# Softmax passes of a graph network: in TensorE's order a step's picks move ahead of the sums of the second group

## The chip, the cores and the metric

The kernel is one program on one core of a Trainium2 chip. The metric is the device time of the whole program in microseconds (us); less is better. A core has TensorE (matrix products; its weight loads are listed apart as PEld), VectorE (DVE), ScalarE (ACT), GpSimd (POOL) and SyncE (SP, which issues transfers). Each engine takes its instructions in the order of its program, and they are tied together by semaphores.

## The reference

Four graph networks run one after the other over the same 3125 nodes and 103,125 edges, which come sorted by destination. Each is followed by a residual sum and a layer norm. The third is the one that matters here. It has three layers, each of them graph attention with 8 heads, a batch norm and a SiLU:

```python
def _gat(x, src, dst, W, a_src, a_dst, bias, n_nodes):
    H, C = a_src.shape
    xw = (x @ W).reshape(n_nodes, H, C)
    al_s = jnp.einsum('nhc,hc->nh', xw, a_src)
    al_d = jnp.einsum('nhc,hc->nh', xw, a_dst)
    logits = jax.nn.leaky_relu(al_s[src] + al_d[dst], LRELU_SLOPE)
    m = jax.lax.stop_gradient(jax.ops.segment_max(logits, dst, num_segments=n_nodes))
    e = jnp.exp(logits - m[dst])
    denom = jax.ops.segment_sum(e, dst, num_segments=n_nodes)
    alpha = e / denom[dst]
    out = jax.ops.segment_sum(alpha[:, :, None] * xw[src], dst, num_segments=n_nodes)
    return out.reshape(n_nodes, H * C) + bias
```

The first two layers have 256 output columns (C = 32), the third 128 (C = 16). All data is fp32.

## The kernel before, in words

The sorted edges are cut into groups of 512 edges that all point into one block of 128 nodes. There are 228 groups; a step takes two of them (1024 edges, 8 tiles of 128), so that a layer's softmax pass (`gat_pass`) has 114 steps, and the three layers have 342. Everything of a step is a chain over four engines:

- POOL (`gather`, L1502) fetches the rows of the source nodes, 8 indirect transfers, two steps ahead of the step whose messages need them.
- ACT (`pack`, L1546) copies the logits' source part out of them. TensorE (`turn`, L1703) transposes it, so that edges lie along the free axis, and DVE (`scan`, L1585) takes a running maximum over each run of edges with one destination. TensorE (`turn_back`, L1709) transposes the maxima back.
- DVE (`run_ends`, L1592) keeps only the value at the end of each run in `ends`. TensorE (`pick`, L1719) multiplies `hot`, the one-hot matrix of the edges' destinations (`edge_hot`, L1577), with `ends`: 8 products of 9 columns, by which each node gets its maximum.
- DVE (`maxima`, L1600 to L1629) raises the running maximum of each node (`top`), works out by how much older sums must fade, and splits al_d and the maximum into three bf16 parts.
- TensorE (`dst_gather`, L1731) brings these parts back to the edges. DVE (`logits`, L1635 to L1644) forms the shifted logits, ACT (`power`, L1558) their exponentials, and DVE (`messages`, L1651) multiplies them into the gathered rows.
- TensorE (`sums(0)` and `sums(1)`, both L1741) sums the messages per node: for each of the two groups of the step 4 products of 264 columns (136 in the third layer) into a PSUM bank of its own. DVE (`add(0)` and `add(1)`) first scales the accumulator of the group's block by the fade (L1673) and then adds the bank (L1677).

The steps overlap. `pipeline` runs one loop on each engine. Its parts carry a lag: in turn t of the loop a part with lag l works on step t - l. The order of the parts in the list is the order of the instructions on that engine, and it is written by hand. In the profile an fp32 product has two records, so that 8 picks are x16 and the 4 products of a group are x8.

DVE's list, and what TensorE has to have finished for its parts:

```python
pipeline(dve, (2, maxima), (1, scan), (2, logits), (1, run_ends), (2, keep_fade), (3, add(0)), (2, messages),
         (3, add(1)), (0, edge_hot), per_turn=RING)
```

`maxima` waits for the picks of its step (made in the turn before), `logits` for `dst_gather` of the same turn, `run_ends` for `turn_back` of the same turn, `add(0)` and `add(1)` for `sums(0)` and `sums(1)` of the same turn. TensorE's parts wait in return: `sums` for the messages of the turn before and for the bank, `dst_gather` for the last instruction of `maxima`, `turn_back` for `scan`, and `pick` for four things:

```python
pe.wait_ge(hot_made, n.total(1, 1))
pe.wait_ge(masked, n.total(1, 2))
pe.wait_ge(flagged, n.total(1, 1))
pe.wait_ge(offered, n.total(1, 1))
```

`masked` is raised by `run_ends` of the same turn. `hot_made`, `flagged` (ACT, L1540) and `offered` (L1603, by which the bank of the picks is free) belong to earlier work.

Of the kernel before, what the change touches and what calls it, by code (L numbers as in the profile page):

```python
# [633 lines left out]
def pipeline(eng, *parts, per_turn=2):  # L634


    last = max(lag for lag, _ in parts)
    head = -(-last // per_turn) * per_turn
    whole = STEPS // per_turn * per_turn

    def at(times):
        for t in times:
            for lag, part in parts:
                if 0 <= t - lag < STEPS:
                    part(Step(None, (t - lag) // per_turn, (t - lag) % per_turn, per_turn))

    at(range(head))
    with eng.Fori(head // per_turn, whole // per_turn) as turn:
        for r in range(per_turn):
            for lag, part in parts:  # L650
                part(Step(turn, (r - lag) // per_turn, (r - lag) % per_turn, per_turn))
    at(range(whole, STEPS + last))
# [794 lines left out]
def gat_pass(nc, m, layer):  # L1447


    _, c, wide, full, both = gat_columns(layer)  # L1450
    RING, TWO = 4, 2
    ROWS = BATCH * HEADS
    with Stage(nc, f"gat{layer}") as st:
# [35 lines left out]
        def blocks_of(eng, n):  # L1489
            _, ids = nc.values_load_multi_w_load_instructions(m.block_tab[0:1, n.group(size=PAIR)], engines=[eng.engine],  # L1490
                                                              min_val=0, max_val=NB - 1)
            return ids

        with nc.Block() as block:
            @block.gpsimd
            def _(pool):
                def gather(n):
                    pool.wait_ge(index_in[n.q], n.count(16, 16))
                    pool.wait_ge(msg_made, n.total(1, 1))
                    pool.sem_inc(passed, 1)  # L1500
                    for j in range(BATCH):
                        pool.indirect_dma_start(rows[n.q][:, j, :], None, table,  # L1502
                                                bass.IndirectOffsetOnAxis(ap=index[n.q][:, j:j + 1], axis=0))\
                            .then_inc(gathered[n.q], 16)

                pipeline(pool, (0, gather), per_turn=RING)
# [189 lines left out]
            @block.tensor  # L1696
            def _(pe):
                def turn(n):
                    q = n.of(TWO)
                    pe.wait_ge(packed, n.total(1, 1))  # L1700
                    pe.wait_ge(scanned, n.total(1, TWO))
                    pe.sem_inc(turn_passed, 1)
                    pe.transpose(turn_ps[0:ROWS, 0:P], al_s[q][:, :, :].rearrange("p b h -> p (b h)"), m.ident[:, :]).then_inc(turned, 1)  # L1703

                def turn_back(n):
                    q = n.of(TWO)
                    pe.wait_ge(scanned, n.total(1, TWO + 1))
                    pe.wait_ge(masked, n.total(1, 1))
                    pe.matmul(back_ps[:, 0:ROWS], run_max[q][:, :], m.ident[0:ROWS, 0:ROWS], start=True, stop=True)\  # L1709
                        .then_inc(backed, 1)  # L1710

                def pick(n):
                    q = n.of(TWO)
# [4 lines that stand above are left out]
                    for j in range(BATCH):  # L1718
                        ins = pe.matmul(pick_ps[:, j * (HEADS + 1):(j + 1) * (HEADS + 1)], hot[n.q][:, j, :], ends[q][:, j, :],  # L1719
                                        start=True, stop=True)  # L1720
                    ins.then_inc(picked, 1)

                def dst_gather(n):
                    q = n.of(TWO)
                    size = PARTS * 2 * HEADS
                    pe.wait_ge(dst_hot[q], n.seen(TWO, 1, 1))
                    pe.wait_ge(shown, n.total(1, 1))
                    pe.wait_ge(parted, n.total(1, 1))
                    pe.wait_ge(joined, n.total(1, 1))
                    for j in range(BATCH):  # L1730
                        ins = pe.matmul(row_ps[:, j * size:(j + 1) * size], dhot[q][:, j * P:(j + 1) * P],  # L1731
                                        parts[q][:, j // GROUP, :, :].rearrange("p k h -> p (k h)"), start=True, stop=True)
                    ins.then_inc(dst_rows, 1)

                def sums(g):
                    def part(n):
                        q = n.of(TWO)
                        pe.wait_ge(msg_made, n.total(1, RING + 1))
                        pe.wait_ge(added, n.total(PAIR, g + 1))
                        for j in range(GROUP):  # L1740
                            ins = pe.matmul(sum_ps[g][:, 0:wide], hot[n.q][:, g * GROUP + j, :], msg[q][:, g * GROUP + j, :],  # L1741
                                            start=j == 0, stop=j == GROUP - 1)
                        ins.then_inc(summed, 1)
                    return part

                pe.sem_inc(turned, RING)
                pe.sem_inc(backed, TWO)
                pe.sem_inc(picked, TWO)
                pe.sem_inc(dst_rows, TWO)
                pe.sem_inc(summed, PAIR * RING)  # L1750
                pipeline(pe, (1, turn), (3, sums(0)), (2, dst_gather), (1, turn_back), (3, sums(1)), (1, pick), per_turn=RING)


def destination_gather(pe, m, n, dhot, table, width, bank, done):
# [326 lines left out]
```

## Time and profile before

| what | value |
|---|---|
| median of 3 runs | 10514.31 us (10507.37 to 10517.66) |
| the profiled execution | 10513.72 us, of which the span is 10511.4 us |
| TensorE, matrix products busy | 7135.4 us (68%) |
| VectorE busy | 5278.9 us (50%) |
| GpSimd busy | 6605.8 us (63%) |
| ScalarE busy | 1896.1 us (18%) |
| softmax passes, first to last `turn_back` | 4868.8 to 9071.8 us, the layers' node work between them |
| mean granted clock of TensorE over the span | 0.626 of full speed |

The span runs from the first to the last instruction; 2.3 us lie around it. The shares are means over stages that have different limits, so the softmax passes have to be read by themselves. The three passes fill some 40% of the span. A granted clock of 1.0 is 2.4 GHz, one of 0.5 is 1.2 GHz.

### The profile page before, as it was taken

The page shows a single profiled execution, that of the slowest core. Times are in us where ns is not written, and L with a number is a line of the kernel's source. Part 1 is how long each engine was busy: PE and PEld are TensorE (multiplying, and loading weights), DVE is VectorE, ACT ScalarE, POOL GpSimd, SP SyncE. Part 2 cuts the span into 40 slices and gives each one's busy share as a digit, 9 for nine tenths or more (in the row PEclk, how much of TensorE's full clock was granted, in tenths as well). Part 3 has the DMA queues.
Part 4 walks back from the last instruction along what each step waited for, and adds up shares of the span by engine and source line. Part 5 has one row for each costly group of instructions (what it writes and reads, how often), then busy time and mean ns, then how long its engine had stood idle before and what let it go on. Part 6 is the DMA issues. An engine that isn't in the chain of part 4 may idle for free. (4 is left out here: it accounts for less than half of the span.)

```text
span 10511.4 us, 139346 instructions
## 1 busy us (share of the span) xinstructions
PE 7135.4 (68%) x31465; PEld 6194.0 (59%) x31466; DVE 5278.9 (50%) x13681; ACT 1896.1 (18%) x4610; POOL 6605.8 (63%) x6850
## 2 busy tenths in 40 slices
PE   0266666666665555547888877888877888688887
PEld 0256565555553444434666655666666777678887
DVE  1233332333332222234777765777756777544444
ACT  0000000000001111112222222222223333222222
POOL 0277775777773777713666634666627777367776
PEclk9855655555556777755666676666665555555555
DMA  0122221222221222203444423444424444244443
GB/s 9 43 58 59 57 59 40 62 59 57 58 54 38 60 60 60 60 21 97 142 141 141 141 85 119 141 141 141 141 64 111 113 111 113 56 116 120 120 120 102
DMA packets 685282, 917.39 MB, mean 87 GB/s; under 512 B 429785, under 2 KB 469403, under 8 KB 685094
## 3 DMA queue, kind: packets, MB, share of 16 engines
q0 software_dynamic: 233472, 500.97, 18.5%
q1 hardware_dynamic: 450726, 414.73, 13.2%
q10 hardware_dynamic: 1024, 1.05, 0.0%
q8 instruction: 18, 0.29, 0.0%
q14 instruction: 42, 0.34, 0.0%
HBM read 899.55 MB, written 17.37 MB: 87 GB/s over the span
## 5 line engine op out<-in xcount | busy, mean ns | idle before, releaser
L1502 POOL DMA_INDIRECT gat_rows<-xw_table,gat_index x2736 | 2590.4, 947 | 1933.8 <-issue 824.6
L1741 PE MATMUL bank<-gat_msg_s,gat_hot 128*128 128x264 f32 (+1 forms) x5472 | 1918.2, 522 | 106.7 <-DVE gat_msg_s L1651 106.6
L1741 PEld LDWEIGHTS bank<-gat_msg_s,gat_hot 128*128 128x128 f32 x5472 | 1394.9, 296 | 377.7 <-issue 110.7
L828 PE MATMUL bank<-gcn_rel,gcn_rhot 100*128 100x64 f32 x3648 | 836.3, 424 | 1019.7 <-DVE gcn_rhot L794 1019.7
L828 PEld LDWEIGHTS bank<-gcn_rel,gcn_rhot 100*128 100x128 f32 x3648 | 794.5, 330 | 1077.2 <-issue 588.3
L683 POOL DMA_INDIRECT gcn_rows<-x_table,gcn_index x912 | 1017.0, 1115 | 276.5 <-issue 257.0
L683 POOL DMA_INDIRECT gcn_rows<-in_x,gcn_index x912 | 1007.7, 1105 | 276.7 <-issue 257.4
L683 POOL DMA_INDIRECT msg_rows<-pre_table,msg_index x912 | 945.9, 1037 | 277.4 <-issue 258.2
L683 POOL DMA_INDIRECT att_rows<-pre_table,att_index x912 | 943.1, 1034 | 276.8 <-issue 254.2
L1719 PEld LDWEIGHTS bank<-gat_ends_s,gat_hot 128*128 128x128 f32 x5472 | 1004.3, 276 | 37.4 <-issue 4.2
L1719 PE MATMUL bank<-gat_ends_s,gat_hot 128*128 128x9 f32 x5472 | 950.1, 312 | 3.3 <-DVE gat_ends_s L1592 3.3
L802 DVE TENSOR_TENSOR gcn_comp_s<-gcn_rows,bank 128x512 f32<-128x512 f32 x228 | 156.7, 687 | 1453.6 <-DMA gcn_rows<-in_x,gcn_index 728.5
L730 PE MATMUL bank<-gcn_msg_s,gcn_hot 128*128 128x128 f32 x3648 | 821.9, 417 | 23.8 <-DVE acc L742 23.8
L730 PEld LDWEIGHTS bank<-gcn_msg_s,gcn_hot 128*128 128x128 f32 x3648 | 785.6, 326 | 24.8 <-issue 24.8
L730 PE MATMUL bank<-msg_msg_s,msg_hot 128*128 128x129 f32 x1824 | 411.8, 416 | 547.2 <-ACT msg_msg_s L1082 547.2
L730 PEld LDWEIGHTS bank<-msg_msg_s,msg_hot 128*128 128x128 f32 x1824 | 381.3, 318 | 574.0 <-DVE acc L742 553.8
L1651 DVE TENSOR_TENSOR gat_msg_s<-gat_rows,bank 128x2112 f32<-128x2112 f32 (+1 forms) x342 | 680.8, 1991 | 0.4 <-issue 0.4
L1098 DVE TENSOR_TENSOR msg_pre_s<-msg_rows,bank 128x512 f32<-128x512 f32 x228 | 146.4, 683 | 856.5 <-DMA msg_rows<-pre_table,msg_index 850.9
L1731 PEld LDWEIGHTS bank<-gat_parts,gat_dhot 128*128 128x128 bf16 x2736 | 128.3, 113 | 740.0 <-issue 738.8
L1731 PE MATMUL bank<-gat_parts,gat_dhot 128*128 128x48 bf16 x2736 | 160.7, 210 | 581.9 <-DVE gat_parts L1629 415.2
L1759 PE MATMUL bank<-kvq,att_dhot 128*128 x1824 | 418.4, 424 | 148.6 <-ACT att_dhot L716 115.1
L1759 PEld LDWEIGHTS bank<-kvq,att_dhot 128*128 128x128 f32 x1824 | 397.6, 330 | 181.6 <-issue 181.6
(293 smaller groups left out, 10442.0 us busy)
## 6 DMA issues: line engine op xcount, KB each, us to landing
gat_dst<-dst_rows SPq DMA_DIRECT2D x342, 512.0 KB
gcn_ids<-rel_rows SPq DMA_DIRECT2D x228, 400.0 KB
att_dst<-dst_rows SPq DMA_DIRECT2D x114, 512.0 KB, 4.0
gat_rows<-xw_table,gat_index POOLq DMA_INDIRECT x2736
att_attr<-in_edge_attr SPq DMA_DIRECT2D x228, 128.0 KB
gcn_rows<-in_x,gcn_index POOLq DMA_INDIRECT x912
gcn_rows<-x_table,gcn_index POOLq DMA_INDIRECT x912
msg_rows<-pre_table,msg_index POOLq DMA_INDIRECT x912
```

Of the source, the lines that this page charges most:

```text
L683: pool.indirect_dma_start(self.rows[n.q][:, j, :], None, self.table, bass.IndirectOffsetOnAxis(ap=self.index[n.q][:, j:j + 1], axis=0))\
L730: ins = pe.matmul(place(banks, g, width), hot[:, g * GROUP + j, :], msg[:, g * GROUP + j, 0:width], start=j == 0, stop=j == GROUP - 1)
L802: dve.tensor_tensor(comp[q][:, :, :], g.rows[q][:, :, :], rel_ps[q][:, :].rearrange("p (b d) -> p b d", b=BATCH), ALU.mult)\
L828: ins = pe.matmul(rel_ps[q][:, j * DIM:(j + 1) * DIM], rhot[q][:, j * P:(j + 1) * P], rel[:, :], start=True, stop=True)
L1098: dve.tensor_tensor(pre[q][:, part, :], g.rows[q][:, part, :], edge_ps[q][i][:, :].rearrange("p (j d) -> p j d", j=GROUP), ALU.add)\
L1502: pool.indirect_dma_start(rows[n.q][:, j, :], None, table, bass.IndirectOffsetOnAxis(ap=index[n.q][:, j:j + 1], axis=0))\
L1651: dve.tensor_tensor(msg[q][:, :, :].rearrange("p b (h e) -> p b h e", h=HEADS), rows[n.q][:, :, 0:wide].rearrange("p b (h e) -> p b h e", ...
L1719: ins = pe.matmul(pick_ps[:, j * (HEADS + 1):(j + 1) * (HEADS + 1)], hot[n.q][:, j, :], ends[q][:, j, :], start=True, stop=True)
L1731: ins = pe.matmul(row_ps[:, j * size:(j + 1) * size], dhot[q][:, j * P:(j + 1) * P], parts[q][:, j // GROUP, :, :].rearrange("p k h -> p ( ...
L1741: ins = pe.matmul(sum_ps[g][:, 0:wide], hot[n.q][:, g * GROUP + j, :], msg[q][:, g * GROUP + j, :], start=j == 0, stop=j == GROUP - 1)
L1759: ins = pe.matmul(bank[:, j * width:(j + 1) * width], dhot[:, j * P:(j + 1) * P], table[:, ds(b, 1), :].rearrange("p o w -> p (o w)"), sta ...
```

## The change

Only the order of TensorE's parts in `gat_pass` changes. `pick` (lag 1) and `sums(1)` (lag 3) trade places, so that a turn runs turn, sums(0), dst_gather, turn_back, pick, sums(1). No instruction is added or taken away, and no wait is changed.

```diff
@@ -1748,7 +1748,7 @@
                 pe.sem_inc(picked, TWO)
                 pe.sem_inc(dst_rows, TWO)
                 pe.sem_inc(summed, PAIR * RING)
-                pipeline(pe, (1, turn), (3, sums(0)), (2, dst_gather), (1, turn_back), (3, sums(1)), (1, pick), per_turn=RING)
+                pipeline(pe, (1, turn), (3, sums(0)), (2, dst_gather), (1, turn_back), (1, pick), (3, sums(1)), per_turn=RING)
```

## Rows read from the trace of the kernel before

**Rows 1.** Busy time by stretch in the first and third softmax pass, and granted clock.
```profile
core 0: us, PE busy (x) PEld busy (x) DVE busy (x) ACT busy (x) POOL busy (x), PEclk, DMA share, GB/s
5000.00:6200.00 1200.00, 976.20 (x4358) 784.09 (x4357) 944.00 (x2837) 353.40 (x1016) 761.51 (x804) 0.69 0.48 141
...
8000.00:9000.00 1000.00, 823.19 (x4176) 777.41 (x4177) 752.91 (x2719) 337.14 (x970) 738.11 (x783) 0.50 0.41 112
```

**Rows 2.** The same view for the messages (L1651) alone: DVE busy, times.
```profile
5000.00:6200.00 1200.00, 237.29 (x102) 0.69 0.48 141
...
8000.00:9000.00 1000.00, 124.09 (x97) 0.50 0.41 112
```

**Rows 3.** DVE's waits from 4850 to 9100 us: total us, times, longest.
```profile
DVE acc L1673 <- issue: 376.3, 340, 1.4
DVE gat_drow L1635 <- PE bank L1731: 119.0, 316, 3.3
...
DVE gat_pen L1600 <- PE bank L1719: 9.0, 5, 2.6
...
DVE acc L1677 <- PE bank L1741: 7.2, 6, 1.9
```

**Rows 4.** Timeline, first layer, DVE: start, us, instruction, xcount, idle before.
```profile
5224.76 0.56 DVE L1635 TENSOR_REDUCE gat_drow<-bank 128x128 f32<-128x384 f32 x1 [0.23 <-PE bank L1731]
...
5226.04 0.22 DVE L1592 TENSOR_TENSOR gat_ends_s<-bank,run_end 128x64 f32<-128x64 f32 x1
...
5228.32 2.35 DVE L1651 TENSOR_TENSOR gat_msg_s<-gat_rows,bank 128x2112 f32<-128x2112 f32 x1
...
5231.11 0.43 DVE L1677 TENSOR_TENSOR acc<-acc,bank 128x264 f32 x1
5231.45 1.22 DVE L1577 TENSOR_TENSOR gat_hot<-bank,dst_l 128x1024 f32<-128x1024 f32 x1
```

**Rows 5.** Timeline, first layer, TensorE, parts of several turns.
```profile
5224.37 0.36 PE L1731 MATMUL bank<-gat_parts,gat_dhot 128*128 128x48 bf16 x8 [1.46 <-DVE gat_parts L1629]
...
5225.02 2.05 PE L1741 MATMUL bank<-gat_msg_s,gat_hot 128*128 128x264 f32 x8
...
5230.80 3.88 PE L1741 MATMUL bank<-gat_msg_s,gat_hot 128*128 128x264 f32 x8 [1.45 <-DVE gat_msg_s L1651]
...
5237.30 3.41 PE L1741 MATMUL bank<-gat_msg_s,gat_hot 128*128 128x264 f32 x8
5240.55 1.85 PE L1719 MATMUL bank<-gat_ends_s,gat_hot 128*128 128x9 f32 x16
5242.25 0.28 PE L1703 MATMUL bank<-ident,gat_al_s 128*64 128x128 f32 x1
...
5272.58 3.89 PE L1741 MATMUL bank<-gat_msg_s,gat_hot 128*128 128x264 f32 x8
5276.26 3.42 PE L1719 MATMUL bank<-gat_ends_s,gat_hot 128*128 128x9 f32 x16
```

**Rows 6.** Timeline, third layer, TensorE and DVE, one turn.
```profile
8309.65 0.47 PE L1731 MATMUL bank<-gat_parts,gat_dhot 128*128 128x48 bf16 x8 [2.01 <-issue]
...
8310.16 0.56 DVE L1635 TENSOR_REDUCE gat_drow<-bank 128x128 f32<-128x384 f32 x1 [0.18 <-PE bank L1731]
...
8310.67 2.18 PE L1741 MATMUL bank<-gat_msg_s,gat_hot 128*128 128x136 f32 x8
...
8311.57 0.23 DVE L1592 TENSOR_TENSOR gat_ends_s<-bank,run_end 128x64 f32<-128x64 f32 x1
...
8312.64 3.42 PE L1719 MATMUL bank<-gat_ends_s,gat_hot 128*128 128x9 f32 x16
...
8315.17 0.30 DVE L1677 TENSOR_TENSOR acc<-acc,bank 128x136 f32 x1
...
8315.91 0.40 PE L1703 MATMUL bank<-ident,gat_al_s 128*64 128x128 f32 x1
...
8316.11 2.02 PE L1741 MATMUL bank<-gat_msg_s,gat_hot 128*128 128x136 f32 x8
```

## The prediction

> **What bounds the kernel now.** I first read busy time by stretch inside the three softmax passes [rows 1], since the means over the whole span mix stages. In the first pass TensorE is busy 976 of 1200 us and DVE 944; in the third 823 and 753 of 1000. None is full, so the view doesn't yet name a bound. The same view for the messages alone gives the number of turns [rows 2]: 102 in 1200 us is 11.8 us a turn, 97 in 1000 us is 10.3 us.
>
> Next I read DVE's waits over all three passes [rows 3]. The largest is "issue" before L1673, 376.3 us in 340 turns, 1.1 us each: DVE waits there for no other engine. The only steady wait for TensorE is that of the logits for `dst_gather`, 119.0 us over some 340 turns, 0.35 us each. For picks DVE waited 5 times (9.0 us), for sums 6 times (7.2 us). So DVE, in its written order, sets the length of a turn, and TensorE delivers both picks and sums before DVE comes to them. TensorE is the one that waits: 1.46 us before `dst_gather` and 1.45 us before `sums(0)` [rows 5]. The question is therefore not what TensorE gains in free time, but whether each of its results is still there when DVE wants it.
>
> Last I read the timeline around the two parts that trade places [rows 4 to 6]. In the first layer `sums(1)` runs right behind `turn_back`, from 5225.02 for 2.05 us, so it ends at 5227.07; `add(1)` takes it at 5231.11, 4.0 us later. In the third layer it ends at 8310.67 + 2.18 = 8312.85 and is taken at 8315.17, 2.3 us later. The picks end last on TensorE in a turn, and nothing waits for them until `maxima` of the next turn.
>
> **The change part by part.** It adds and removes no instruction and no transfer, and alters no wait; the two parts keep their durations at a given clock. What moves is where waits stand in TensorE's queue.
>
> 1. *The picks have to wait where they stood free.* `pick` needs `masked`, which `run_ends` (L1592) raises in the same turn. DVE does `run_ends` behind the logits; it ends at 5226.04 + 0.22 = 5226.26 in the first layer and at 8311.80 in the third [rows 4, 6]. TensorE is through with `turn_back` when `sums(1)` starts now, at 5225.02 and 8310.67. So TensorE stands still for some 1.2 us a turn where it works on sums today. The other three waits of `pick` (the one-hot matrix, ACT's flags, the free bank) are for work of the turn before or of the head of this one, and cost nothing. ACT, POOL and SP don't come into it: no queue of theirs is reordered.
>
> 2. *`sums(1)` comes behind that wait and behind the picks.* I count from the end of `run_ends`. To `add(1)` it is 5231.11 - 5226.26 = 4.85 us in the first two layers, and 8315.17 - 8311.80 = 3.37 us in the third. That much time TensorE has for both parts. It needs:
>  - the handover from DVE to TensorE, 0.13 us (messages end at 5230.67, the sums that wait for them start at 5230.80 [rows 4, 5]); I take 0.1;
>  - the picks, start to the next part's start: 8315.91 - 8312.64 = 3.27 us at 1.2 GHz [rows 6], 5242.25 - 5240.55 = 1.70 us at 2.4 GHz [rows 5];
>  - `sums(1)` to its end: 3.89 us at the low clock and 2.05 us at the high one in the first two layers [rows 5], 2.18 us at the low clock in the third [rows 6].
>
> 3. *Third layer.* The granted clock is 0.50 throughout [rows 1]. 0.1 + 3.27 + 2.18 = 5.55 us against 3.37: `add(1)` starts 2.2 us later each turn. Behind it on DVE stand `edge_hot` and all of `maxima` of the next turn, hence `dst_gather`, the logits and `run_ends`: the whole loop moves by that much. Both parts run together in 112 of the 114 turns (picks have lag 1, sums lag 3), so 112 x 2.18 = 244 us.
>
> 4. *First and second layer.* Here the granted clock is 0.69 on average, and it depends on it. Both parts slow: 0.1 + 3.27 + 3.89 = 7.26, which is 2.4 us late. Fast picks, slow sums: 5.69, 0.84 late. Slow picks, fast sums: 5.42, 0.57 late. Both fast: 3.85, in time. Which is it? Today the clock goes up behind a long block of sums: slow sums of 3.41 us at 5237.30, then fast picks of 1.85 us at 5240.55 [rows 5]. The picks profit from the sums ahead of them. In the new order they have ahead of them a wait for `maxima`, the short `dst_gather` and `turn_back`, and the wait for `run_ends`. And picks don't raise the clock by themselves, as the third layer shows: there TensorE works almost without a gap from 8309.65 to 8318.13, 8.5 us, and stays at 1.2 GHz [rows 1, 6]. The block that raises it will be `sums(1)`, turn, `sums(0)`, which then stand together; the rise comes in time for `sums(0)`, which nobody is in a hurry for, and will mostly be lost in the two idle stretches that follow. I weigh both slow with 8 in 10 and the two mixed cases with 1 in 10 each: 0.8 x 2.4 + 0.1 x 0.84 + 0.1 x 0.57 = 2.06 us. 2 x 112 turns make 461 us. The ends are 0 (both fast, always) and 2.4 x 224 = 540 us.
>
> The Trainium skill (TensorE: Matmul & The Clock Gate, "Why this matters for your kernels") advises keeping TensorE continuously busy to get the high clock. By it the new block of picks, sums, turn and sums would be fast, and the first two layers would lose nothing, 244 us in all in place of 705. The third layer of this trace speaks against it: 8.5 us of such work stayed slow. I go by the trace and keep the page's outcome as part of a rival.
>
> 5. *Given back.* TensorE must still end `sums(0)` before the next `dst_gather`. At the low clock a turn of it is 1.02 + 1.2 + 0.1 + 3.27 + 3.7 + 0.5 + 3.9 = 13.7 us (`dst_gather` and `turn_back` from 8309.65 to 8310.67, the wait, the handover, the picks, 3.7 for `sums(1)` to the start of the next part by 5272.58 to 5276.26, some 0.5 for turn and its handover, `sums(0)`; [rows 5, 6]), against 11.8 + 2.4 = 14.2 on DVE's side, so DVE keeps the bound, just. The picks are ready earlier, but DVE waited for them 9.0 us in all [rows 3]: no gain. POOL, busy 738 of 1000 us with its gaps of issue beside [rows 1], gets more room in a longer turn.
>
> **Sum.** The profiled execution took 10513.7 us (span 10511.4 and 2.3 around it), 0.6 us under the median of 10514.3. 10513.7 + 244 + 461 = 11,219; I say 11,220 us, 6.7% slower.
>
> **The rivals.**
>
> *The clock mix of today survives* (0.19). The page's rule works in part: the long block keeps the clock up often enough that either the picks or the sums are fast in the first two layers. For it: fast and slow picks both occur today with idle stretches around them [rows 5]. Against it: step 4. With 0.57 to 1.5 us a turn late, 128 to 336 us, and 244 for the third layer, the time is 10,886 to 11,094; about 10,990.
>
> *TensorE becomes a second bound* (0.04). If `dst_gather` has to wait for `sums(0)`, a turn in the first two layers gets still longer than 14.2 us. 0.5 us more is 112 us: 11,330. Against it: the 0.5 us of room in step 5.
>
> *The order doesn't matter* (0.02). `sums(1)` would have to end before DVE wants it in every layer: within 4.85 us, and within 3.37 us in the third. There the slow picks alone with the handover take 3.37, so the clock would have to rise there too. Time 10,514.
>
> *Faster* (0.02). The full clock holds through the whole turn in all three layers. Then picks and sums need 3.85 us in the first two, and in the third about half of 5.55, 2.9, both in time, and the logits no longer wait for a slow `dst_gather`: from its start to L1635 it is 0.39 us when fast [rows 4, 5] and 0.51 us when slow [rows 6]. 0.12 x 336 turns = 40 us: 10,474. It decides only from the point where the third layer leaves 1.2 GHz, which it never does today [rows 1].
>
> **How the numbers follow.** My forecast, both slow in most turns, holds 0.73: with 1.6 to 2.45 us a turn in the first two layers and 2.0 to 2.3 in the third, 10513.7 + 358 + 224 = 11,096 to 10513.7 + 549 + 258 = 11,320. The range for 8 in 10 takes in half of the first rival: 10,960 to 11,330. A difference under 0.2%, some 21 us, can't be told from none in this kernel. All cases but the last two are slower: faster 0.02, same 0.02, slower 0.96.
>
> **What would show it.** In the waits of DVE a new large one stands before L1677, released by TensorE's L1741: some 2.2 us x 112 turns in the third layer and some 2 us x 224 in the others, against 7.2 us now. TensorE waits some 1.2 us before L1719, put down to L1592. In the timeline the order is L1709, gap, L1719, L1741, L1703, L1741. Turns last 12.5 us in the third layer and 13.9 in the first two. The slow picks (3.42 us) are the rule in the first two layers too; if they last 1.85 us mostly, step 4 is wrong and the time is nearer 10,990. If L1677 doesn't wait, step 2 is wrong, and with it the sign.

## The result, and the profile after

The changed kernel takes 11262.08 us in the median (4 runs, 11256.08 to 11264.59) beside 10515.99 us for the kernel before: the ratio is 1.071, 95% interval 1.0692 to 1.0729. The forecast was 11,220 us, range 10,960 to 11,330. One thing has to be known to read what follows: on the chips that ran the experiments e1 to e7, e11 and e12 the kernel before itself took 12,700 to 13,080 us, so each of those runs is compared with before on its own chip, and otherwise by stretches of its trace.

The profiled execution of the changed kernel has a span of 11261.6 us. DVE's waits over the three passes, which answer to [rows 3]:

```profile
DVE acc L1677 <- PE bank L1741: 821.5, 342, 2.7
DVE acc L1673 <- issue: 376.3, 340, 1.4
...
DVE gat_drow L1635 <- PE bank L1731: 85.1, 265, 3.4
...
DVE gat_pen L1600 <- PE bank L1719: 8.1, 4, 2.6
```

The wait of `add(1)` for `sums(1)` has grown from 7.2 us to 821.5 us, 2.4 us in each of 342 turns. What else DVE waits for inside the passes is as before or a little less: the 1.1 us of issue before L1673 are the same 376.3 us, and the logits wait 34 us less for `dst_gather`.

The timeline of TensorE in the first layer (answers to [rows 5]; columns as there):

```profile
5209.93 0.36 PE L1731 MATMUL bank<-gat_parts,gat_dhot 128*128 128x48 bf16 x8 [2.73 <-DVE gat_parts L1629]
5210.22 0.43 PE L1709 MATMUL bank<-ident,gat_run_max 64*128 64x64 f32 x2
5212.02 3.32 PE L1719 MATMUL bank<-gat_ends_s,gat_hot 128*128 128x9 f32 x16 [1.37 <-issue]
5215.19 3.87 PE L1741 MATMUL bank<-gat_msg_s,gat_hot 128*128 128x264 f32 x8
5218.85 0.41 PE L1703 MATMUL bank<-ident,gat_al_s 128*64 128x128 f32 x1
5219.06 1.98 PE L1741 MATMUL bank<-gat_msg_s,gat_hot 128*128 128x264 f32 x8
5223.96 0.36 PE L1731 MATMUL bank<-gat_parts,gat_dhot 128*128 128x48 bf16 x8 [2.92 <-DVE gat_parts L1629]
```

And DVE in the same turn (answers to [rows 4]):

```profile
5211.69 0.23 DVE L1592 TENSOR_TENSOR gat_ends_s<-bank,run_end 128x64 f32<-128x64 f32 x1
...
5219.10 0.43 DVE L1677 TENSOR_TENSOR acc<-acc,bank 128x264 f32 x1 [2.44 <-PE bank L1741]
5219.44 1.22 DVE L1577 TENSOR_TENSOR gat_hot<-bank,dst_l 128x1024 f32<-128x1024 f32 x1
```

`run_ends` is over at 5211.92, the picks start at 5212.02, `sums(1)` at 5215.19 and ends at 5219.06, and DVE takes it at 5219.10: 7.18 us behind `run_ends`, where before it was 4.85. The picks and the first sums run at 1.2 GHz or nearly so (3.32 and 3.87 us, where at 1.2 GHz throughout they take 3.4 to 3.6 and 3.87 to 3.89 in both kernels); only the sums behind them, which are `sums(0)` and for which nobody waits, run at 2.4 GHz (1.98 us). TensorE then stands for 2.9 us, until DVE's `maxima` is through.

This turn is not an exception. In the 85 turns of 5000 to 6200 us the picks take 2.77 to 3.56 us, `sums(1)` 3.40 to 3.87, and the wait of L1677 is 1.88 to 2.68 us long, 2.44 in the mean. In each of them DVE starts L1677 0.03 or 0.04 us behind the end of `sums(1)`. The trace also has a turn in the second layer in which the picks were fast:

```profile
6691.60 1.92 PE L1719 MATMUL bank<-gat_ends_s,gat_hot 128*128 128x9 f32 x16 [1.33 <-issue]
6693.38 3.60 PE L1741 MATMUL bank<-gat_msg_s,gat_hot 128*128 128x264 f32 x8
6697.01 0.43 DVE L1677 TENSOR_TENSOR acc<-acc,bank 128x264 f32 x1 [0.76 <-PE bank L1741]
```

Picks and sums take 1.92 and 3.60 us here, 1.91 less together than the 3.56 and 3.87 of a turn at 1.2 GHz, and the wait is 0.76 us in place of 2.67: 1.91 less. So their length goes over into the wait one for one. By this row some 1.6 us of a turn's loss in the first two layers are the picks' low clock (an estimate: 3.56 - 1.92). Of the 214 turns of these two layers that I could read, 2 have picks under 2.5 us, both in the second layer.

A turn of the third layer (answers to [rows 6]), TensorE:

```profile
8702.86 3.56 PE L1719 MATMUL bank<-gat_ends_s,gat_hot 128*128 128x9 f32 x16 [1.12 <-issue]
8706.27 2.16 PE L1741 MATMUL bank<-gat_msg_s,gat_hot 128*128 128x136 f32 x8
8708.22 0.42 PE L1703 MATMUL bank<-ident,gat_al_s 128*64 128x128 f32 x1
```

and DVE:

```profile
8708.47 0.30 DVE L1677 TENSOR_TENSOR acc<-acc,bank 128x136 f32 x1 [2.43 <-PE bank L1741]
```

The turns' lengths follow from one line per stretch, the messages alone (us of the stretch, DVE busy, times; answers to [rows 2]):

```profile
5000.00:6200.00 1200.00, 201.60 (x86) 0.71 0.41 119
8500.00:9500.00 1000.00, 102.37 (x80) 0.58 0.34 92
```

From the first to the last start of these messages it is 5002.2 to 6197.9 us over 85 turns and 8503.3 to 9497.0 over 79: 14.07 and 12.58 us a turn. Before it was 5003.3 to 6199.7 over 101 and 8004.1 to 8993.5 over 96: 11.85 and 10.31. In the second layer the same reading gives 14.03 us (6666.5 to 7844.7 over 84) against 11.86 (6567.7 to 7599.6 over 87). The differences, (2.22 + 2.17 + 2.27) x 112 = 746 us, are the whole loss (746 us).

### The profile page after: what moved, and what is told of

It is laid out like the page before. It is cut to its first block and busy times, and to the rows that moved or that the text cites. A ratio compares the mean times of both kernels' runs of the same rounds, so it can differ in the third digit from the quotient of the medians.

```text
span 11261.6 us, 139346 instructions
## 1 busy us (share of the span) xinstructions
PE 7226.2 (64%) x31465; PEld 6312.9 (56%) x31466; DVE 5275.9 (47%) x13681; ACT 1895.6 (17%) x4610; POOL 6617.5 (59%) x6850
## 5 line engine op out<-in xcount | busy, mean ns | idle before, releaser
L1741 PE MATMUL bank<-gat_msg_s,gat_hot 128*128 128x264 f32 (+1 forms) x5472 | 1829.0, 504 | 10.3 <-DVE gat_msg_s L1651 10.3
L1719 PE MATMUL bank<-gat_ends_s,gat_hot 128*128 128x9 f32 x5472 | 1183.0, 355 | 412.9 <-issue 409.6
L1719 PEld LDWEIGHTS bank<-gat_ends_s,gat_hot 128*128 128x128 f32 x5472 | 1160.3, 322 | 457.2 <-issue 457.2
L1731 PE MATMUL bank<-gat_parts,gat_dhot 128*128 128x48 bf16 x2736 | 135.8, 192 | 937.7 <-DVE gat_parts L1629 692.0
L1651 DVE TENSOR_TENSOR gat_msg_s<-gat_rows,bank 128x2112 f32<-128x2112 f32 (+1 forms) x342 | 680.9, 1991 | 0.4 <-issue 0.4
L1677 DVE TENSOR_TENSOR acc<-acc,bank 128x264 f32 (+1 forms) x684 | 263.2, 385 | 851.6 <-PE bank L1741 821.5
```

The costliest lines, as they stand in the source:

```text
L1651: dve.tensor_tensor(msg[q][:, :, :].rearrange("p b (h e) -> p b h e", h=HEADS), rows[n.q][:, :, 0:wide].rearrange("p b (h e) -> p b h e", ...
L1677: dve.tensor_tensor(dst_acc, dst_acc, sum_ps[g][:, 0:wide].unsqueeze(1), ALU.add).then_inc(added, 1)
```

## The experiments

**The changed kernel and the kernel before, again (e8, e9).** No edit; they give a second chip for the main result, and the measure for e10.

> The changed kernel itself, unaltered, beside the kernel before on a chip where before takes some 12,700 to 13,100 us. The undisturbed turns should be those of the first comparison: 13.9 us in the first two layers, 12.4 in the third. In turns that are stretched by late instructions of TensorE, part of the 2.2 us is covered. Theory: the ratio is 1.03 to 1.057 (400 to 746 us). If the ratio is under 1.01, the loss belongs to the first chip's timing and not to the order.

> The kernel before, unaltered, for its trace on this chip: the measure for the turns of the other experiments. The shortest quarter of its turns should lie at 11.7 us and 10.2 us, as in the trace shown first; what stretches the others should be gaps of TensorE put down to issue, and results of TensorE that reach DVE late.

On this chip before takes 10490.37 us and nothing is stretched. The changed kernel takes 11230.99 us, ratio 1.0704 (1.0686 to 1.0722). The expectation of 1.03 to 1.057 had reckoned with a stretched chip and doesn't meet this case; the loss is the full one, so it isn't the first chip's alone. The changed kernel by itself was never timed on a chip where before takes 12,700 us or more. The kernel before gave 10490.4 us in its profiled execution; its turns are 11.85 and 10.31 us in the mean, as in the trace shown first, and none of the stretching that e9 was to explain is there.

**Work that needs no sums put into the wait (e10).** The changed kernel, and in DVE's list:

```diff
 ...
-(3, add(0)), (2, messages), (3, add(1)), (0, edge_hot)
+(3, add(0)), (2, messages), (0, edge_hot), (3, add(1))
```

> The changed kernel with DVE's edge_hot ahead of add(1), so that 1.2 us of work that needs no sums lie in the wait. Theory (DVE stands before add(1), in its own order): the wait of L1677 falls from 2.4 to some 1.3 us a turn in undisturbed turns. The loads of the block numbers for maxima then stand behind a short instruction and show some 0.8 us of issue before L1600, so that the turn shrinks by 0.2 to 1.0 us: 13.0 to 13.8 us in the first two layers. Rival (TensorE's own row of work sets the turn): the wait of L1677 stays at 2.4 us less nothing, and the turn gets no shorter, or 0.7 us longer.

It takes 11187.87 us, ratio 1.0663 (1.0646 to 1.0681), 43 us less than the changed kernel on the same chip. DVE's waits in the first layer, 5000 to 6200 us, first of e10:

```profile
DVE acc L1677 <- PE bank L1741: 116.3, 87, 1.5
...
DVE gat_pen L1600 <- issue: 82.5, 87, 1.3
```

then of e8, the changed kernel:

```profile
DVE acc L1677 <- PE bank L1741: 210.1, 86, 2.7
...
DVE gat_pen L1600 <- issue: 6.7, 22, 0.3
```

The wait falls from 2.44 to 1.34 us a turn, by 1.1 us, as `edge_hot` is 1.2 us long. Of that some 0.9 us come back as issue before L1600 (82.5 us in 87 turns, where e8 has 6.7 us): `maxima` loads its block numbers there, and `edge_hot` no longer stands just ahead of it. Net 43 / 336 = 0.13 us a turn, less than the 0.2 to 1.0 expected. TensorE's program is the same in both, and `sums(1)` is taken at the same distance behind `run_ends` (7.20 us in the mean, 7.18 in the changed kernel of the result); what DVE does before it asks for the bank shortens the wait. The fall of the wait alone doesn't rule out that TensorE's own row of work sets the turn, since a gain of 0.13 us is near to none. TensorE's waits rule it out: in the changed kernel it stands for 1.3 us before the picks and for 2.7 us before `dst_gather`, in every turn, and both times for DVE.

**The wait without the picks (e1, e5).** The kernel before, with a part `await_ends` that only waits:

```diff
 ...
-(1, turn_back), (3, sums(1)), (1, pick)
+(1, turn_back), (1, await_ends), (3, sums(1)), (1, pick)
 ...
+def await_ends(n):
+    pe.wait_ge(masked, n.total(1, 2))
```

> The order of before, but TensorE waits for run_ends (masked) ahead of sums(1); the picks stay behind the sums. The wait of the change without its swap. Theory (DVE's add(1) has to wait for sums(1) only because the slow picks stand ahead of it): sums(1) now ends 0.1 + 3.89 = 4.0 us behind run_ends, inside the 4.85 us that DVE leaves (third layer 2.3 of 3.37), so L1677 doesn't wait. The picks end later instead, at 7.2 us at the low clock, where maxima wants them at 6.7 (third layer 5.5 against 4.9): some 0.5 us a turn in perhaps half of the 336 turns. 10,600 us, 10,520 to 10,700, far under 11,262. Rival (it is TensorE standing still for 1.2 us a turn that costs, whatever comes behind it): the same 2.2 us a turn as in the changed kernel, about 11,250.

> The same kernel as e1, since on the chip of that call the kernel before itself took 13,080 us and its turns were stretched by waits that the runs shown first don't have. Where the kernel before takes 10,515 us the theory gives, as for e1, 10,600 us (10,520 to 10,700) and no wait of L1677 for sums; the rival, by which TensorE's standing still costs by itself, about 11,250.

Beside before on the same chips it is no slower: 12914.16 us, ratio 0.9885 (0.983 to 0.9939), and 12721.17 us, ratio 0.9998 (0.9969 to 1.0026). As ratios the theory had said 1.01 and the rival 1.07; both lie above the intervals, the rival far above. The changed kernel by itself has no time on these chips; the nearest is e3 below, the changed order with filling, with 1.0267 on the chip of e1. DVE in a turn of e5 without long gaps:

```profile
6907.12 0.22 DVE L1592 TENSOR_TENSOR gat_ends_s<-bank,run_end 128x64 f32<-128x64 f32 x1
...
6912.51 0.43 DVE L1677 TENSOR_TENSOR acc<-acc,bank 128x264 f32 x1
6914.53 0.17 DVE L1600 TENSOR_SCALAR gat_pen<-bank 128x8 f32<-128x8 f32 x1 [0.46 <-PE bank L1722]
```

and TensorE, where the sums of `sums(1)` stand on L1744 and the picks on L1722:

```profile
6907.39 3.89 PE L1744 MATMUL bank<-gat_msg_s,gat_hot 128*128 128x264 f32 x8 [1.20 <-DVE gat_ends_s L1592]
6911.07 3.42 PE L1722 MATMUL bank<-gat_ends_s,gat_hot 128*128 128x9 f32 x16
```

TensorE stands for 1.20 us, about as long as in the changed kernel, and runs at the low clock too. `sums(1)` ends at 6911.28, and L1677 starts at 6912.51 without waiting. What is late now are the picks, by 0.46 us. Between 5800 and 7000 us of e5, L1677 waits in 25 of 73 turns (60.9 us), and in the others not at all; long waits in some of the turns are there in e4 too, which has TensorE's order of before. In e3 and e11, which have the changed order, it waits in all 66 turns of the same stretch (174.0 and 172.2 us). So the wait for `run_ends` by itself costs next to nothing here; it is the wait with the picks behind it.

**Half of the picks ahead (e2, e6).** `pick` cut in two, 4 of the 8 products in each part:

```diff
 ...
-(1, turn_back), (3, sums(1)), (1, pick)
+(1, turn_back), (1, pick_first), (3, sums(1)), (1, pick_rest)
```

> Turn_back, the waits of pick, 4 of the 8 picks, sums(1), the other 4 picks. Theory: what stands ahead of sums(1) counts by its length. sums(1) ends at 0.1 + 1.64 + 3.8 = 5.5 us against 4.85, 0.7 late; third layer 0.1 + 1.64 + 2.18 = 3.9 against 3.37, 0.55 late: 224 x 0.7 + 112 x 0.6 = 224 us, so 10,740 us (10,650 to 10,850), less than a third of the change's loss. Rival (TensorE's idle time itself): all of it, about 11,250. Rival (a loss in proportion to the picks moved): half, 10,890.

> The same kernel as e2, for the same reason. Theory (what stands ahead of sums(1) counts by its length against the room that DVE leaves): 10,740 us (10,650 to 10,850), with L1677 waiting some 0.6 us a turn. Rival by idle time: about 11,250. Rival in proportion to the picks moved: 10,890.

12664.63 us, ratio 0.9691 (0.9637 to 0.9745), and 12491.42 us, ratio 0.9824 (0.9775 to 0.9873): on these chips faster than before, where the theory had said a ratio of 1.02 and both rivals more. As forecasts of the time all three failed, and why it gains isn't settled. What the trace does show is the wait. A turn of e6 in the first layer, TensorE (L1715 the picks, L1747 the sums):

```profile
6799.45 1.85 PE L1715 MATMUL bank<-gat_ends_s,gat_hot 128*128 128x9 f32 x8 [1.34 <-issue]
6801.15 3.87 PE L1747 MATMUL bank<-gat_msg_s,gat_hot 128*128 128x264 f32 x8
```

and DVE:

```profile
6805.05 0.43 DVE L1677 TENSOR_TENSOR acc<-acc,bank 128x264 f32 x1 [1.01 <-PE bank L1747]
```

With half the picks ahead, 1.85 us, L1677 waits 1.01 us, where all of them, 3.3 us, make it 2.4 us, and none of them none. In the turns around it the wait is 0.53, 0 and 1.02 us, which is the some 0.6 us expected; in the turn without a wait the half took 1.29 us and the sums 3.44. The picks' length goes over into the wait as soon as the room is used up, as the theory has it.

**The clock (e3, e11).** The changed kernel with products that nobody reads in TensorE's gaps: 5 and 2 in e3, 7 and 3 in e11.

```diff
 def pick(n):
 ...
+    pe.wait_ge(offered, n.total(1, 1))
+    fill(pick_ps, 3)
 ...
     pe.wait_ge(masked, n.total(1, 2))
 ...
 def dst_gather(n):
 ...
+    pe.wait_ge(joined, n.total(1, 1))
+    fill(row_ps, 7)
     pe.wait_ge(dst_hot[q], n.seen(TWO, 1, 1))
```

The waits for `offered` and `joined`, by which the two banks are free, move ahead of the filling.

> The changed kernel, with products into unused columns of TensorE's own banks that nobody reads: 5 of 128 columns ahead of dst_gather's wait for maxima, 2 ahead of pick's wait for run_ends. No work of the chain is changed. Theory: of the 2.2 us a turn the greater part is the low clock at which the picks and sums(1) run behind two idle stretches. With the stretches filled the clock should stay at 1.0 in the first two layers: 0.1 + 1.70 + 2.05 = 3.85 against 4.85, no wait at L1677, and at full clock in the third about 2.9 against 3.37. About 10,520 us; if the clock rises in part only, up to 10,900. Rival (the order costs by the positions of the waits, whatever the clock): 11,260 or more, since TensorE has more to do.

> As e3, with more filling: in the changed kernel, 7 products of 128 columns that nobody reads ahead of dst_gather's wait and 3 ahead of the wait of the picks, which is some 1.8 and 0.8 us at the high clock, in gaps of 2.9 and 1.3 us. Theory (without the low clock the picks and sums(1) fit in the room that DVE leaves): the clock stays near 1.0, L1677 waits for next to nothing, 10,500 to 10,600 us where before takes 10,500. If the clock rises in part, 10,600 to 10,950. Rival (positions alone, whatever the clock): as the changed kernel, 11,230 us, or more by the filling.

13428.79 us, ratio 1.0267 (1.0205 to 1.0329), and 13463.95 us, ratio 1.0334 (1.0281 to 1.0387). This is neither the theory's time nor an answer for it. TensorE in e11 (L1714 the filling, L1724 the picks):

```profile
6519.54 0.36 PE L1737 MATMUL bank<-gat_parts,gat_dhot 128*128 128x48 bf16 x8 [0.20 <-issue]
...
6520.19 0.94 PE L1714 MATMUL bank<-ones,ident 128*128 128x128 f32 x6
6525.65 3.55 PE L1724 MATMUL bank<-gat_ends_s,gat_hot 128*128 128x9 f32 x16 [4.53 <-issue]
```

and DVE:

```profile
6524.04 0.56 DVE L1635 TENSOR_REDUCE gat_drow<-bank 128x128 f32<-128x384 f32 x1 [4.33 <-remote]
```

The filling ran at the high clock (6 records in 0.94 us), but DVE saw the result of `dst_gather` 4.3 us late, and in that gap the clock fell again: the picks took 3.55 us as ever. The chip alone doesn't explain this lateness. DVE's waits from 5800 to 7000 us, first in e3, then in e1 on the same chip, without filling:

```profile
DVE gat_drow L1635 <- remote: 272.0, 65, 4.9
```

```profile
DVE gat_drow L1635 <- PE bank L1734: 19.0, 67, 0.4
```

It stands in all but one turn of e3 and likewise in e11 (277.1 us in 65), while e1 has it in 3 turns (8.7 us). So it came with the filling, or with the filling on such a chip. Why is open. What the filling was to test, fast picks in every turn, was therefore not measured; the only evidence is the turns of the changed kernel in which the picks happened to be faster, shown under the result.

**Block numbers of `add` loaded early (e4, e7, e12).** The order of before; on DVE a part `add_ids` with the load ahead of `maxima`:

```diff
-pipeline(dve, (2, maxima), (1, scan),
+pipeline(dve, (3, add_ids), (2, maxima), (1, scan),
 ...
```

> The order of before. DVE loads the two block numbers of add at the head of the turn, ahead of maxima, behind edge_hot's 1.2 us, in place of right ahead of add(0), where 1.1 us a turn stand as issue. Theory (DVE's own list sets the turn): up to 1 us a turn less in the first two layers, until TensorE, which waits for DVE some 2 us of 11.8, or GpSimd sets it; in the third GpSimd has 8 x 1.25 = 10.0 of 10.3 us, so little: 10,514 - 0.8 x 224 - 0.2 x 112 = 10,310 us (10,270 to 10,500). Rival (TensorE bounds the turn already): no change.

> The same kernel as e4 (the order of before; DVE loads add's two block numbers at the head of the turn), again because the kernel before took 13,080 us beside e4. Theory (DVE's own list sets the turn): where before takes 10,515 us, 10,310 us (10,270 to 10,500); turns of the first two layers 10.9 to 11.5 us against 11.8. Rival (TensorE bounds the turn already): no change.

> As e4 and e7, which gave ratios of 0.981 and 0.980 on chips where before took some 13,070 us: the order of before, with add's block numbers loaded at the head of the turn. Where before takes 10,500 us: turns of 11.4 to 11.7 us in the first two layers (what the shortest quarter showed in e4 and e7, against 11.5 to 11.75 of before), so the gain is 0.1 to 0.4 us a turn: 10,400 to 10,480 us. If DVE alone set the turn it would be 1 us a turn and 10,230.

12801.05, 12785.54 and 12793.28 us, with ratios of 0.9806 (0.9751 to 0.9861), 0.9798 (0.9758 to 0.9837) and 0.9814 (0.9764 to 0.9864). It beat the kernel before three times, by 2%, the ratio that e4's theory had for it, but only on chips where before takes some 13,000 us; where before takes 10,500 us it wasn't measured. The 1.1 us of issue before L1673 went, and 0.76 us of it came back before `maxima`. Two turns of e12, the picks and L1600 in each:

```profile
6961.18 1.85 PE L1720 MATMUL bank<-gat_ends_s,gat_hot 128*128 128x9 f32 x16
6965.03 0.17 DVE L1600 TENSOR_SCALAR gat_pen<-bank 128x8 f32<-128x8 f32 x1 [0.76 <-issue]
...
6973.00 3.42 PE L1720 MATMUL bank<-gat_ends_s,gat_hot 128*128 128x9 f32 x16
6976.64 0.17 DVE L1600 TENSOR_SCALAR gat_pen<-bank 128x8 f32<-128x8 f32 x1 [0.76 <-PE bank L1720]
```

The second wait is put down to the picks, which end at 6976.42. But in the turn before they were over at 6963.03, 2.0 us early, and the same 0.76 us stand there as issue. So it is the loads, now twice as many behind `edge_hot`, that take this time; that TensorE would be the next bound close behind is not shown.

## Why the prediction was right

*Step 1, the picks have to wait.* Right: 1.37 us before L1719 in the turn shown of the first layer and 1.26 in the mean, 1.12 in the third, against 1.2 forecast. I had said that the profile would put it down to L1592; it puts it down to issue. That the picks start 0.1 us behind `run_ends` in every turn shows the releaser.

*Step 2, the count from `run_ends`.* The mechanism is right, one term was too small. Where both parts run at 1.2 GHz the count is 7.41 us, not 7.26, and in the third layer 5.70, not 5.55. The picks take 3.41 us to the next part's start (8702.86 to 8706.27), where I had 3.27 from the kernel before. That the turn shown comes to 7.18 is because its picks are a little faster. e5 and e6 agree that neither the wait alone nor the number of products decides, but the length ahead of `sums(1)` against the room that DVE leaves.

*Step 3, third layer.* 2.18 us forecast, 2.27 measured: 254 us for 244. `add(1)` is 5.70 - 3.37 = 2.33 us later, and the logits wait 0.05 us less.

*Step 4, first two layers.* The mechanism is right, the weights were too mild: 2.06 us forecast, 2.22 and 2.17 measured, 492 us for 461. I had given the mixed cases 2 turns in 10; of the 85 turns of 5000 to 6200 us none has fast picks or a fast `sums(1)`. So `add(1)` is 7.18 - 4.85 = 2.33 us later in the mean, 0.27 more than forecast, and 0.11 of it came back at the logits. That the number lies so near is in part luck: two misses with opposite signs. The price of a mixed case was right: fast picks with slow sums were to make `add(1)` 0.84 us late, and in the turn at 6691.60 L1677 waits 0.76. The rise came where step 4 had put it, in time for `sums(0)`.

The Trainium skill advises keeping TensorE busy to get the high clock (TensorE: Matmul & The Clock Gate, "Why this matters for your kernels"). This trace doesn't agree. In the third layer the granted clock rose from 0.50 to 0.58 although TensorE was busy for less of the time, 674.67 of 1000 us where it was 823.19 [rows 1]:

```profile
8500.00:9500.00 1000.00, 674.67 (x3421) 634.44 (x3422) 615.22 (x2222) 277.86 (x799) 600.56 (x635) 0.58 0.34 92
```

The rise came too late for what DVE waits for: `sums(1)` still takes 2.16 us there, in all of 95 turns.

*Step 5, given back.* DVE kept the bound, by more than I had worked out. TensorE was to stand for only 0.5 us before `dst_gather`; it stands for 2.7 us in the mean (waits of TensorE, 5000 to 6200 us, 85 turns), because `sums(0)` runs fast, 2 to 3 us in place of 3.9:

```profile
PE bank L1731 <- DVE gat_parts L1629: 165.4, 64, 3.1
...
PE bank L1731 <- issue: 62.8, 21, 3.3
```

What was given back I had put at nothing. The waits of L1677 sum to 821.5 us, 814 more than before, and the loss is 746. The logits' wait fell from 119.0 to 85.1 us, because `dst_gather` runs at the high clock more often (busy 135.8 us in all, 160.7 before). This is the small gain that the rival "faster" had named, 34 us for its 40. Another 0.1 us a turn, some 34 us, is no loss: that much lies between L1673 and L1677 even without a wait (5213.09 + 0.43 to 5213.62 in the same turn), and the profile counts it into the wait.

*The rivals.* Clock mix of today: no, as step 4 says. Second bound: no, by TensorE's 2.7 us. GpSimd isn't a bound either: in the first layer it waits for DVE's messages 362.4 us over 86 turns, in the third 219.3 us over 80. No change and faster: no.

## What to carry to other kernels

Free time on an engine is no room for a reordering. What counts is, for each result, how long before its consumer comes it is ready today, against what the new neighbour ahead of it takes, with the neighbour's own wait counted in, and at the clock that it will run at. A part whose consumer comes in this turn belongs ahead of one whose consumer comes in the next. And where an engine in order waits, fill the wait with its own later work only after looking at what that work hid until then: in e10 nearly the whole gain of 1.1 us went into a load that `edge_hot` had covered, and in e12 the same loads came back at another place.

## What the hardware showed that was not expected

On the chips of e1 to e7, e11 and e12 the same program took up to 25% longer (13,080 against 10,490 us), also outside the softmax passes. The trace of e5 in the first pass over the edges has stretches in which TensorE's instructions come one by one, start to start 1.4 to 2.8 us apart, with nothing to wait for that the profile shows:

```profile
730.83 0.26 PE L828 MATMUL bank<-gcn_rel,gcn_rhot 100*128 100x64 f32 x1 [1.74 <-issue]
...
732.24 0.26 PE L828 MATMUL bank<-gcn_rel,gcn_rhot 100*128 100x64 f32 x1 [1.15 <-issue]
...
735.03 0.26 PE L828 MATMUL bank<-gcn_rel,gcn_rhot 100*128 100x64 f32 x1 [2.52 <-issue]
```

Late delivery of the instructions would look like this, but nothing here shows it, and what sets these chips apart stays open. Half of the picks ahead, which was to cost 2%, gained 2 to 3% there. So a result from such a chip can't be taken over to one without these gaps unless it is measured there, and the 2% of the early loads stand under the same reserve.
